# Normalising, turning and projecting the second attention layer's x in parts of 2, 4 and 2 batches instead of two halves

## The reference, cut to what matters

```python
x = x + _L0_xattn_ref(_layernorm(x, axis=-1), ctx_1024, ...)      # 16 heads of 16, 375 context rows, biases
x = x + _L0_ffn_ref(_layernorm(x, axis=-1), ...)                  # 8 experts, the best 2 of each row
x = x + _L1_xattn_ref(_layernorm(x, axis=-1), ctx_1024, L1_xattn_Wq, L1_xattn_Wkv, L1_xattn_Wout, mask_SxS2_fk0)
x = x + _L1_ffn_ref(_layernorm(x, axis=-1), ...)
```

```python
q = query @ Wq.T                                   # query: the normalised x
k, v = jnp.split(context @ Wkv.T, 2, axis=-1)
scores = jnp.einsum('bqha,bkha->bqkh', q, k) + mask[None, :, :, None]
attn = jax.nn.softmax(scores * scale, axis=2)
out = jnp.einsum('bqkh,bkha->bqha', attn, v).reshape(b, q_len, d)
return out @ Wout.T
```

## Time and profile before

| what | value |
| --- | --- |
| median of 3 runs | 653.61 us (652.04 to 654.36) |
| the profiled execution's own time | 651.84 us |
| its span in the trace | 650.1 us |
| PE busy | 547.0 us, 84% of the span, 5314 matmuls |
| DVE busy | 367.3 us, 56% |
| ACT busy | 364.1 us, 56% |
| POOL busy | 152.0 us, 23% |

### The profile page before, as it was taken

How to read it: one execution, slowest core, us unless ns; L and a number is a source line. 1 busy time by engine, 2 the same in 40 slices (tenths; PEclk the granted TensorE clock), 3 DMA queues, 4 the chain that set the end, 5 groups by cost and what they waited for, 6 DMA issues and landing times. The chain is left out here.

```text
span 650.1 us, 14727 instructions
## 1 busy us (share of the span) xinstructions
PE 547.0 (84%) x5314; PEld 468.1 (72%) x5314; DVE 367.3 (56%) x1122; ACT 364.1 (56%) x862; POOL 152.0 (23%) x238
## 2 busy tenths in 40 slices
PE   2898999999884279999999986879999999757646
PEld 2777878887773169999999975668888888546525
DVE  3677676666754601141222107598776667569784
ACT  2668788778763022233323313588978787645462
POOL 2031543434315141111111006503021222020000
PEclk9989999999998579999999997799999999968778
DMA  6372102112002997557555405300011110000001
GB/s 160 137 200 73 48 28 72 50 48 78 3 11 82 367 331 258 197 181 257 192 176 171 146 24 152 105 2 19 32 50 49 49 50 3 1 3 1 0 1 57
DMA packets 33514, 62.80 MB, mean 97 GB/s; under 512 B 4146, under 2 KB 24451, under 8 KB 33316
## 3 DMA queue, kind: packets, MB, share of 16 engines
q1 hardware_dynamic: 29700, 47.97, 22.6%
q0 software_dynamic: 2928, 10.75, 5.8%
q10 hardware_dynamic: 816, 3.15, 1.3%
HBM read 51.11 MB, written 10.75 MB: 95 GB/s over the span
## 5 line engine op out<-in xcount | busy, mean ns | idle before, releaser
L1466 ACT ACTIVATE ex_h_t<-ex_h,b_e 128x128 f32<-128x128 f32 x168 | 48.0, 368 | 125.1 <-PE ex_h L1650 125.1
L1082 PEld LDWEIGHTS a_ring<-ident,w_all 112*125 112x125 f32 x768 | 88.7, 188 | 23.4 <-issue 13.0
L1082 PE MATMUL a_ring<-ident,w_all 112*125 112x112 f32 x768 | 100.1, 280 | 6.0 <-ACT w_all L575 5.9
L583 ACT ACTIVATE w_all<-a_ring 125x448 f32<-125x448 f32 x128 | 62.8, 542 | 45.6 <-PE a_ring L1082 45.6
L1650 PE MATMUL ex_h<-ex_xg_t,w_s 128*128 128x128 f32 x672 | 80.0, 278 | 0.4 <-issue 0.4
L810 DVE CUSTOM_DVE_ANT_0 w_all<-a_s,mask_sb 112x375 f32<-112x375 f32 x128 | 65.3, 543 | 24.5 <-issue 13.4
L1650 PEld LDWEIGHTS ex_h<-ex_xg_t,w_s 128*128 128x128 f32 x672 | 78.3, 195 | 0.6 <-issue 0.6
L803 DVE TENSOR_REDUCE a_mx<-a_s 112x2 f32<-112x750 f32 x64 | 59.6, 931 | 30.3 <-PE a_s L1073 30.3
L1669 PE MATMUL ex_y<-w_all,ex_h_t 128*128 x336 | 75.9, 379 | 0.0
L575 ACT ACTIVATE w_all<-w_all,a_shift 112x375 f32<-112x375 f32 x128 | 68.8, 600 | 3.8 <-DVE a_shift L815 2.7
L1572 DVE TENSOR_TENSOR ex_y_sb<-ex_y,b_all 128x256 f32<-128x256 f32 x21 | 8.9, 425 | 104.6 <-PE ex_y L1669 104.5
(11 more groups left out here) (276 smaller groups left out, 798.6 us busy)
## 6 DMA issues: line engine op xcount, KB each, us to landing
w_s<-in_L_ffn_W SPq DMA_DIRECT2D x18, 1024.0 KB, 5.5
w_all<-in_L_ffn_W SPq DMA_DIRECT2D x8, 1024.0 KB, 11.7
ct_dram<-a_ct SPq DMA_DIRECT2D x8, 752.0 KB, 4.4
a_ct<-ct_dram POOLq DMA_DIRECT2D x8, 752.0 KB
w_s<-in_L_ffn_W ACTq DMA_DIRECT2D x3, 1024.0 KB, 11.3
w_all<-in_ctx SPq DMA_DIRECT2D x8, 375.0 KB
y_slots<-ex_y_sb SPq DMA_DIRECT2D x21, 128.0 KB, 1.7
w_ud<-in_L_ffn_w SPq DMA_DIRECT2D x2, 1024.0 KB, 9.4
```

Of the source, the lines that this page charges most:

```text
L583: a.activation(et[:, t % 2, kc], bank("et", t, kc)[0:KP, 0:4 * S], ACT.Copy)\
L1082: last = nc.tensor.transpose(bank("et", t, kc)[0:KP, r * S:(r + 1) * S], es[:, t % 2, r, kc * KP:(kc + 1) * KP], ident[0:S, 0:S])
L1466: last = a.activation(h_t[:, i % 2, f], hb[i % 2][:, f * 128:(f + 1) * 128], ACT.Gelu, bias=b1_e[:, i % 2, f:f + 1])
```

## The change

The second layer's batches are cut in three parts, parts = (0, 2, 6, B): batches 0 and 1, then 2 to 5, then 6 and 7. Each part has its own moments, deviation, normalising, xt and queries. A table steps says in which step a part's xt is made; its moments stand two steps ahead, its normalising one step ahead, its queries one and two steps behind.

- Lead-in: only combined(0), combined(1) and the work of part 0 (224 columns instead of 448).
- Step -1: combined(2) and (3). Step 0: combined(4) and (5). Step 3: combined(6) and (7).
- Part 1 (448 columns): moments in step 1, normalising in 2, xt in 3, queries in 4 and 5.
- Part 2 (224 columns): moments in step 6, normalising in 7, xt in 8, queries in 9 and 10.
- Query products of a part of 224 columns are 256 columns wide; POOL zeroes the 32 columns behind the 224 with a memset at the very start of its stream, and PE's first query product waits for it.
- POOL's deviation(n) stands at the head of its stream's step steps - 2, ahead of output(b-1) and keys(b+1, 1) of the same step.

The first layer has steps = {2: 1} and parts = (0, 4, B), which gives the order that it had.

```diff
-                parts = (0, 4, B) if first else (0, 3, 4, B)
+
+                parts = (0, 4, B) if first else (0, 2, 6, B)
+
+                steps = {late + 2: 1} if first else {3: 1, 8: 2}
...
-                    order += {2: [("xt", 1, 0), ("xt", 1, 1)], 3: [("q", 1, 0)], 4: [("q", 1, 1)]}.get(t - late, [])
+                    for ago, m in ((0, None), (1, 0), (2, 1)):
+                        if t - ago in steps:
+                            n = steps[t - ago]
+                            order += [("xt", n, 0), ("xt", n, 1)] if m is None else [("q", n, m)]
...
+                            g_.memset(xnt[:, :, :, 2 * S:256].bitcast(F32), 0.0).then_inc(padded, 1)
                             load_turned(0)
...
                         if not first:
-                            deviation(1)
                             for b in range(4, B):
                                 gather(b)
                         for t in range(-1, NQ + 4):
                             b, g = divmod(t, 4)
-                            if t == late:
-                                deviation(len(parts) - 2)
+                            if t + 2 in steps:
+                                deviation(steps[t + 2])
...
                             combined(1)
-                            combined(2)
                             moments(0)
-                            combined(3)
-                            moments(1)
                             normal(0)
-                            normal(1)
...
-                            if not first and 0 <= t < 4:
-                                combined(4 + t)
-                            if t == late:
-                                moments(len(parts) - 2)
-                            if t == late + 1:
-                                normal(len(parts) - 2)
+                            if not first and t in (-1, 0, 3):
+                                combined(2 * t + 4 if t <= 0 else 6)
+                                combined(2 * t + 5 if t <= 0 else 7)
+                            if t + 2 in steps:
+                                moments(steps[t + 2])
+                            if t + 1 in steps:
+                                normal(steps[t + 1])
...
-                            at = 2 * (DC * (b // 4) + c) + 2
+                            at = 2 * (DC * part_of(b) + c) + 2
```

More of the change, by code:

```diff
@@ L540, in values, with normal @@
                             a.activation(dst, src, ACT.Copy).then_inc(is_read("v", b, n), 1)
[L542 to L553, removed]
+                        def normal(n, c):
+                            wait_filled(act, "xt", n, c)
+                            if n:
+                                wait_filled(act, "q", n - 1, 1)
+                            a.activation(xnt[:, 0, c, 0:width(n)], bank("xt", n, c)[:, 0:width(n)], ACT.Copy).then_inc(xt_hi, 1)
@@ L554, in queries @@
+                        def queries(n, m):
+                            wait_filled(act, "q", n, m)
+                            src = bank("q", n, m)[:, 0:width(n)]
+                            dst = qp[:, 0, m, 0:width(n)]
+                            if n:
+                                act.wait_ge(qz_even, 2 * (DC * (n - 1) + m) + 2)
+                                act.wait_ge(qz_odd, 2 * (DC * (n - 1) + m) + 2)
                             if mask is None:
-                                a.activation(qp[:, 0, m], src, ACT.Identity, bias=b_col[:, m:m + 1]).then_inc(q_hi, 1)
+                                a.activation(dst, src, ACT.Identity, bias=b_col[:, m:m + 1]).then_inc(q_hi, 1)
@@ L671, in _ @@
                                 context(b + 2, 1)
[L672 to L680, removed]
+                            if t in steps:
+                                normal(steps[t], 0)
+                                normal(steps[t], 1)
+                            for m in range(DC):
+                                if t - 1 - m in steps:
+                                    queries(steps[t - 1 - m], m)
+                                    odd_heads(steps[t - 1 - m], m)
                             if not first:
@@ L1041, in values, with turned_x, queries @@
                             last.then_inc(is_filled("v", b, n), 1)
[L1043 to L1054, removed]
+                        def turned_x(n, c):
+                            pe.wait_ge(xn_out, parts[n + 1])
+                            wait_free(pe, "xt", n, c)
+                            for i, b in enumerate(range(parts[n], parts[n + 1])):
+                                last = nc.tensor.transpose(bank("xt", n, c)[:, i * S:(i + 1) * S],
+                                                           xn[:, b, c * 128:(c + 1) * 128], ident[0:S, 0:S])
+                            last.then_inc(is_filled("xt", n, c), 1)
+                        def queries(n, m):
+                            wait_read(pe, "xt", n, 0)
+                            wait_read(pe, "xt", n, 1)
+                            wait_free(pe, "q", n, m)
+                            if not first and n == 0:
+                                pe.wait_ge(padded, 1)
                             ms = slice(m * 128, (m + 1) * 128)
-                            product(bank("q", half, m)[:, 0:HALF], [(wr[:, 0, 0, k, ms], wr[:, 1, 0, k, ms]) for k in range(DC)],
-                                    [(xnt[:, 0, k], xnt[:, 1, k]) for k in range(DC)]).then_inc(is_filled("q", half, m), 1)
+                            w = max(width(n), 256)
+                            product(bank("q", n, m)[:, 0:w], [(wr[:, 0, 0, k, ms], wr[:, 1, 0, k, ms]) for k in range(DC)],
+                                    [(xnt[:, 0, k, 0:w], xnt[:, 1, k, 0:w]) for k in range(DC)]).then_inc(is_filled("q", n, m), 1)
                         def scores(t):
@@ L1246, in _ @@
                                     output(b - 1)
-                            if t == late + 2:
-                                turned_x(1, 0)
-                                turned_x(1, 1)
-                            if t == late + 3:
-                                queries(1, 0)
-                            if t == late + 4:
-                                queries(1, 1)
+                            if t in steps:
+                                turned_x(steps[t], 0)
+                                turned_x(steps[t], 1)
+                            for m in range(DC):
+                                if t - 1 - m in steps:
+                                    queries(steps[t - 1 - m], m)
                             if not first:
```

64 lines of the change are left out of this document (35 added, 29 removed).

## The result

The changed kernel takes 655.62 us (median of 20 runs, 653.45 to 658.68), the kernel before 653.83 us in the same sessions (20 runs, 651.11 to 656.09). The ratio is 1.0031, 95% interval 1.0017 to 1.0046: 1.8 us slower, inside the predicted range and on the predicted side, but less than half of the predicted +4.1. The profiled executions stand further apart: 656.59 (span 654.9) against 651.84, +4.75.

What follows compares the result with a forecast made beforehand. PE was taken to set the pace in the steady part, DVE in steps 0 to 4. The terms -5.0 + 1.6 + 2.35 + 4.7 + 0.5 gave +4.1 us, on 653.61 a forecast of 657.7 us, range 654.0 to 659.8.

Steps and rivals of the forecast that it cites:

- Lead-in: Second layer up to the first scores: less work ahead of them, -5.0 us.
- Step -1: S(-1) to S(0): combined(2) and (3) now stand at its end, +1.6 us.
- the memset: POOL's memset ahead of the first context load in the lead-in: +0.25 us, between nothing and 1.09.
- Steps 0 to 2: Early steps at DVE's pace: added DVE work makes them 13.73 us instead of 11.38, +2.35.
- Steps 3 to 5: Splitting of xt and part 1's query chain over ACT and DVE: 18.1 us instead of 13.44, +4.7.
- Steps 6 to 11: S(6) to T(12): part 2's queries 2.3 us and a late load 1.3, 31.3 us against 30.8, +0.5.
- T(12): T(t) is PE's start on turning step t; T(12) was to come 4 us later, nothing differing behind step 12.
- The late load: Batch 3's context load, behind part 2's deviation on POOL: PE waits 1.3 us in step 8, bounds nothing to 1.3.
- S(-1): S(t) is DVE's start on the maxima that stand first in step t; S(-1) was 415.92 before.
- Rival 3: The clock falls to 1.2 GHz in steps 0 to 3: +3 us over two steps, 660.8 us; chance 0.08.
- Rival 1: Early steps absorb it: steps 3 to 5 cost 2.7, the load nothing; +0.9, 654.5 us; chance 0.22.
- Rival 2: Lead-in's gain stays: DVE's surplus in steps 0 to 5 is lag made up from step 6; 651.0 us; chance 0.08.

Runs made afterwards that it cites:

- e7: Changed kernel with part 2 one step later (steps {3: 1, 9: 2}) and the deviation at its step's end, behind batch 3's context load: 652.94 us, ratio to before 0.9995.
- before again: The kernel before, unedited, run once more for a second profile: 654.53 us, layer 186.8 us.
- e6: Kernel before with only a memset of 128 numbers a partition added at the start of POOL's stream in the second layer: 654.04 us, ratio 1.0007.
- e11: Kernel before with the gathers of batches 4 to 7 behind the first maxima and batch 2's context load ahead of them: 650.68 us, ratio 0.9999.
- e3: Kernel before with only the second half cut in two, parts (0, 4, 6, B): 654.53 us, ratio to before 1.0013.
- e4: Changed kernel with one combined per step, steps {5: 1, 12: 2} and the deviation at its step's end: 656.86 us, ratio to before 1.0049.
- e8: Changed kernel with parts (0, 2, 4, B), part 2's pieces and queries in steps 12 to 14, deviation at its step's end: 652.64 us, ratio to before 1.0000.
- e10: Changed kernel with part 2 two steps later (steps {3: 1, 10: 2}) and the deviation at its step's end: 651.05 us, ratio to before 1.0012.
- e9: Changed kernel with parts (0, 2, 4, B), part 2's pieces and queries in steps 10 to 12, deviation at its step's end: 649.78 us, ratio to before 0.9991.
- e12: e9 with the gathers of batches 4 to 7 behind the first maxima and batch 2's context load ahead of them: 650.92 us, ratio to before 1.0001.
- e1: The changed kernel, unedited, run again for a second profile: 655.16 us, ratio to before 1.0029.
- e2: Changed kernel with POOL's deviation moved to the end of its step: 655.84 us, ratio to before 1.0027.

## Why the prediction was right in side and too large in size

By its own steps, measured in the profiled pair:

- *Lead-in, -5.0.* First scores 5.26 us sooner. Right; of its items the memset doesn't show. At the maxima only 4.4 remained, because DVE started 0.78 us behind the scores' end, not 0.05, and the scores took 0.12 longer.
- *Step -1, +1.6 (6.8 us).* It took 7.56. The sentence that PE's keys of batch 1 are ready in time held for PE, but not for DVE: its split waits 1.64 us for ACT's copy of them, and combined(2) and (3) stand behind it.
- *Steps 0 to 2, 13.73 us.* 13.72, but step by step 4.66, 4.86 and 4.20 against 4.74, 4.61 and 4.38: two misses that cancel. In step 1 PE is busy all 4.86 us, with the clock at 0.50 for most of it, and DVE 4.50.
- *Steps 3 to 5, 18.1 us.* 18.26. DVE waits for ACT's query copies (1.71 and 1.60 us), as said.
- *Steps 6 to 11, +0.5.* +1.2 by S(6) to T(12) (32.06 us). The late load is there, 1.02 us of PE for the 1.3 I took, and e7 removed it. Unforeseen: in steps 9 and 10 a DVE operation on the queries is held up by POOL, 0.72 and 0.62 us (last section), and in step 10 PE's keys wait 1.10 us for DVE's copy.

The terms add up to +6.4 there, 2.3 more than forecast, and the timed difference is +1.8. So the prediction missed in two opposite directions, and that the time came out inside its range is partly luck. **The step that failed is the base of the first terms.** The prediction takes the lengths of before from one profiled execution. It held S(-1) at 25.3 us behind the layer's start, and three other profiles with that lead-in have 26.9, 27.4 and 27.2. It held steps 0 to 2 at 11.38 us, and these three have 12.6, the 1.2 us of step 1 in which the clock fell. So the forecast +2.35 there is +1.1 against them. By T(12), before again and e6 are 3.2 and 2.9 us behind the first profile. How often the kernel before loses this isn't known: e11, with its order in these steps, doesn't, and isn't timed faster than before. Measured from before again and e6, T(12) moves by 3.2 and 3.5 us to the changed kernel, against a forecast of about 4 and a timed +1.8; the layer starts 387.3 to 390.6 us into the span, a scatter of the same size, and the last 1.4 to 1.7 us stay open.

The rivals. *Rival 3* came in part: the clock fell in steps 0 and 1 in both profiles of the changed kernel. Its price of 3 us fell: steps 0 and 1 are long by DVE's own work, which covers the slower PE but for 0.25 us in step 1. Where the steps are shorter the fall costs 1.2 us (before again, e3, e6) to some 1.5 (e4, e8). *Rival 1* has the size (+1.8 lies in its -2 to +2) but not the mechanism: it said that PE's order absorbs steps 3 to 5, and those steps took their full 18.3 us, and the load was late. *Rival 2*, that DVE's surplus is only lag, is against T(12), and e7 isn't a case of it: it wins its time in steps 8 and 10. The largest term that can be taken away is the late load with its step, 1.7 us timed, nearly the whole loss. What stays then, lead-in gained against slower early steps, shows no gain in four placements (e7 to e10, ratios 0.9991 to 1.0012, every interval with 1 in it).

## What to carry to other kernels

Shortening a lead-in by moving work behind it pays only if the steps that take the work have slack on that engine; here DVE was 97% busy in steps 0 to 4, and against the 5.3 us gained stand 2.4 (step -1), 2.3 (steps 0 to 2) and 4.8 (steps 3 to 5). When work on one queue moves, look at what is queued behind it: a deviation of about 1 us ahead of a 752 KB load made PE wait 1.0 us, and putting it with its part behind the load won 1.7 us, where the third part itself cost some 0.8 (-0.2 to +1.9). And take a base from more than one profile when the sum is below 1% of the time: the two of the kernel before differ by 3.2 us by step 12 of this layer.

## What the runs showed of the hardware

A DVE tensor_scalar on the queries (source and target in SBUF) that starts while POOL splits keys with a tensor_tensor (L409, 0.98 to 1.06 us) doesn't end before it: it ends 0.12 to 0.14 us behind POOL's end. 128x224 elements took 0.94 to 1.09 us instead of 0.33 in all 13 cases, in nine profiles, in which the operation started 0.05 to 0.18 us behind POOL's (470.99 and 478.06 in the changed kernel, 473.57 in e7, 440.95 in e9, and others). DVE's smallest tensor_scalar, the shift of the maxima (112x2, 0.17 us alone), is held in the same way: wherever it starts beside the key split it ends 0.02 to 0.07 us behind it, up to 0.89 us long; it stands on the step's chain, for ACT's exponentials wait for it. These two lines are of the kernel before, which has it as well:

```profile
486.36 0.99 POOL L393 TENSOR_TENSOR a_kp<-a_k_raw,a_kp 128x376 fp32r<-128x376 f32 x1
...
487.02 0.37 DVE L815 TENSOR_SCALAR a_shift<-a_mx 112x2 f32<-112x2 f32 x1
```

The masked maximum itself (L826, 0.54 us) and the splittings that read PSUM (L804) aren't stretched beside the key split; beside a gather the same tensor_scalar grows to 0.44 at most, and beside POOL's 112x2 power not at all (one case, 457.03 in e3). The Trainium skill (SBUF — State Buffer, Terms) says that DVE and GpSimd arbitrate for one shared port pair, held for a full instruction, and that the loser fully blocks. For the key split the trace agrees: DVE's end follows POOL's, and isn't a share of its speed; with the power on 2 elements a partition it shows no block for the full instruction. In e10 no query operation is stretched by a key split, and its layer is 1.8 us shorter than e7's, 0.7 of it DVE's idle time ahead of the first maxima; the times don't confirm that gain.

DVE's idle time between the end of the first scores and the first maxima has three sizes, 0.05 to 0.07 us (before's first profile, e9 to e12), 0.71 to 0.78 (changed, e1, e4, e7, e8) and 1.6 to 2.6 (e2, before again, e3, e6), with nothing named that ends it. The same kernel shows 0.05 in one profile and 2.56 in another. Its cause is open.
